# Graph attention on one core: the additive layers as straight code, with the layer norm written per node tile by ScalarE

## The reference

```python
def _L0_gnn_ref(h, W, a, adj):              # layer 2 is the same
    Wh = jnp.einsum('bni,io->bno', h, W)
    s1, s2 = Wh @ a[:Fout, 0], Wh @ a[Fout:, 0]
    e = leaky_relu(s1[:, :, None] + s2[:, None, :], negative_slope=0.2)
    attention = softmax(e + mask(adj)[None, :, :], axis=2)
    return elu(jnp.einsum('bnm,bmo->bno', attention, Wh))

x = _layernorm(x + _L0_gnn_ref(x, L0_gnn_W, L0_gnn_a, adj), axis=-1)
```

## Time and profile before

| | |
|---|---|
| median of 3 runs | 2508.43 us (2503.49 to 2509.16) |
| profiled execution, its time | 2503.22 us |
| profiled execution, its span | 2501.5 us |
| mean granted TensorE clock | 0.913 of full |
| busy: PE, DVE, ACT, POOL | 2154.4, 1853.4, 1133.6, 871.6 us |

### The profile page before, as it was taken

One profiled execution on the slowest core, in us unless ns is written; L12 is line 12 of the kernel. 1 busy time (PEld: TensorE's weight loads), 2 busy tenths in 40 slices (PEclk: granted clock), 3 DMA queues, 4 the chain that ended last, 5 costly groups with the idle time before them and its releaser, 6 DMA issues.

```text
span 2501.5 us, 56118 instructions
## 1 busy us (share of the span) xinstructions
PE 2154.4 (86%) x22776; PEld 1436.9 (57%) x22776; DVE 1853.4 (74%) x2222; ACT 1133.6 (45%) x1992; POOL 871.6 (35%) x631
## 2 busy tenths in 40 slices
PE   6777756788677774999999999999999999999993
PEld 5666646777466663445545555555555555655552
DVE  5888857988588885767786787786776776788773
ACT  3223224443232231655554555564564565556552
POOL 1655644665466553001221222122122122122124
PEclk8888878989788886999998999999998999999997
DMA  5000000000000000000000000000000000000000
GB/s 136 1 0 0 0 1 1 0 0 1 2 1 0 0 0 4 1 9 2 14 14 2 14 14 2 14 13 4 12 13 6 10 13 6 10 14 10 5 14 18
DMA packets 30720, 23.82 MB, mean 10 GB/s; under 512 B 21776, under 2 KB 25424, under 8 KB 30544
## 3 DMA queue, kind: packets, MB, share of 16 engines
q1 hardware_dynamic: 30544, 21.31, 3.5%
HBM read 8.72 MB, written 4.19 MB: 5 GB/s over the span
## 4 chain that ended last, share of the span: by engine, by line
PE 53%; DVE 4%; issue 2%; POOL 1%; ACT 1%; SPq 0%; DMA 0%; DVEq 0%; ACTq 0%; POOLq 0%
PE fourth_ps_out L1331 18%; PE fourth_ps_scores L1283 6%; PE fourth_ps_out L1345 5%; PE fourth_ps_scores L1286 4%; PE fourth_ps_scores L1289 4%; PE fourth_ps_prep L1244 3%; PE fourth_ps_prep L1259 3%; DVE fourth_weights L983 2%; PE fourth_ps_prep L1251 2%; PE fourth_ps_scores L1307 2%; PE fourth_ps_scores L1313 1%; PE fourth_ps_scores L1310 1%; PE fourth_ps_scores L1316 1%; PE fourth_ps_prep L1234 1%; PE fourth_ps_prep L1212 1%
## 5 line engine op out<-in xcount | busy, mean ns | idle before, releaser
L983 DVE TENSOR_TENSOR fourth_weights<-fourth_weights,keep_mask 128x1024 f32<-128x1024 f32 x512 | 681.7, 1371 | 244.4 <-ACT fourth_weights L1131 243.3
L1131 ACT ACTIVATE fourth_weights<-fourth_ps_scores 128x512 f32<-128x512 f32 x1024 | 529.8, 605 | 467.1 <-PE fourth_ps_scores L1289 466.5
L1331 PE MATMUL fourth_ps_out<-fourth_weights,fourth_x_stage 128*64 128x512 f32 x2048 | 498.3, 606 | 1.1 <-DVE fourth_weights L983 1.1
L1331 PEld LDWEIGHTS fourth_ps_out<-fourth_weights,fourth_x_stage 128*64 128x64 f32 x2048 | 123.0, 136 | 235.4 <-issue 186.9
L1283 PE MATMUL fourth_ps_scores<-fourth_g_high,fourth_x_high 64*128 64x512 f32 x1024 | 234.1, 453 | 22.7 <-issue 20.3
L1283 PEld LDWEIGHTS fourth_ps_scores<-fourth_g_high,fourth_x_high 64*128 64x128 f32 x1024 | 98.4, 188 | 221.4 <-issue 121.6
L1289 PE MATMUL fourth_ps_scores<-fourth_g_low,fourth_x_high 64*128 64x512 f32 x1024 | 206.3, 398 | 0.0
L1286 PE MATMUL fourth_ps_scores<-fourth_g_high,fourth_x_low 64*128 64x512 f32 x1024 | 206.2, 397 | 0.0
L990 DVE TENSOR_TENSOR fourth_weights<-fourth_weights,keep_mask 128x1024 f32<-128x1024 f32 x128 | 153.5, 1237 | 66.7 <-ACT fourth_weights L1138 66.7
L404 DVE SCALAR_TENSOR_TENSOR third_weights<-third_row,third_gain,keep_mask 128x1024 f32<-128x1024 f32 x128 | 185.4, 1461 | 12.7 <-ACT third_row L497 10.8
L404 DVE SCALAR_TENSOR_TENSOR first_weights<-first_row,first_gain,keep_mask 128x1024 f32<-128x1024 f32 x128 | 185.0, 1458 | 12.7 <-ACT first_row L497 11.4
(11 more groups left out here) (267 smaller groups left out, 3532.9 us busy)
## 6 DMA issues: line engine op xcount, KB each, us to landing
setup_adj<-in_adj SPq DMA_DIRECT2D x8, 512.0 KB, 7.5
fourth_h_high<-fourth_h_high SPq DMA_DIRECT2D x32, 128.0 KB, 2.3
fourth_h_low<-fourth_h_low SPq DMA_DIRECT2D x32, 128.0 KB, 2.3
out<-keep_x SPq DMA_DIRECT2D x16, 256.0 KB, 2.6
keep_x<-in_x SPq DMA_DIRECT2D x1, 512.0 KB, 11.4
fourth_bias_rows<-in_L_gnn_bh SPq DMA_DIRECT2D x8, 0.2 KB
fourth_wh_in<-in_L_gnn_Wh SPq DMA_DIRECT2D x2, 32.0 KB
fourth_wo_in<-in_L_gnn_Wo SPq DMA_DIRECT2D x1, 64.0 KB
```

Of the source, the lines that this page charges most:

```text
L983: dve.tensor_tensor(buf[:, :], buf[:, :], keep.mask[:, st.t, :].bitcast(F32), ALU.mult)\
L1131: act.activation(weights[st.slot + g][:, cols(half)], ps_scores[g][:, cols(half)], ACT.Exp)\
L1331: last = pe.matmul(ps_out[rows(half), cols(g)], x_stage[st.s][:, st.t, half, :], weights[st.slot + g][:, cols(half)], start=(st.t == 0), s ...
```

## The change

Only `additive_layer` changes, and the norm that it uses. x is turned where it lies, two tiles at a time (4 transposes for 8), so that even tiles come out in the upper and odd tiles in the lower 64 rows; `x_turned` is half as long, and `stage_x` is gone. The new class `NodeNorm` stands for `LayerNorm` in these two layers: ACT squares and sums each tile in one instruction (`accum_out`) with minus the mean as its bias, and writes the normalised x with eight instructions, with rstd as scale and an offset as bias. DVE's reduce over the squares, POOL's `centre` and POOL's write go. y has two buffers. The loop is written out as 16 steps, and no element 16 is prepared. The order on DVE, ACT and POOL changes. `fill_plain` was on POOL and stays there.

```diff
+    def sum_up_squares(self, act, n):
+        act.wait_ge(self.mean_ready, n)
+        for t in range(TILES):
+            act.activation(self.squares[:, t, :], self.y[n % 2][:, t, :], ACT.Square, bias=self.minus_mean[:, t:t + 1],
+                           accum_out=self.sum_squares[:, t:t + 1]).then_inc(self.sum_squares_ready, 1)
+
+    def variance(self, dve, n):
+        dve.wait_ge(self.sum_squares_ready, TILES * n)
+        dve.tensor_scalar(self.variances[:, :], self.sum_squares[:, :], 1.0 / DIM, EPS, ALU.mult, ALU.add)\
+           .then_inc(self.variance_ready, 1)
+
+    def inverse_deviation(self, pool, n):
+
+        pool.wait_ge(self.variance_ready, n)
+        pool.tensor_tensor(self.rstd[:, :], self.variances[:, :], self.exponent[:, :], ALU.pow)\
+            .then_inc(self.rstd_ready, 1)
+        pool.wait_ge(self.rstd_ready, n)
+        pool.tensor_tensor(self.offset[:, :], self.minus_mean[:, :], self.rstd[:, :], ALU.mult)\
+            .then_inc(self.offset_ready, 1)
+
+    def write(self, act, n, x, x_written):
+        act.wait_ge(self.offset_ready, n)
+        for t in range(TILES):
+            act.activation(x[:, t, :], self.y[n % 2][:, t, :], ACT.Identity, bias=self.offset[:, t:t + 1],
+                           scale=self.rstd[:, t:t + 1]).then_inc(x_written, 1)
```

POOL's program:

```diff
+                scale_values(0, 0)
+                for b in range(BATCH):
+                    if b > 1:
+                        norm.inverse_deviation(pool, b - 1)
+                    if b:
                         residual(b - 1)
                     fill_plain(b)
...
+                    if b + 1 < BATCH:
+                        scale_values(b + 1, (b + 1) % 2)
```

DVE's step:

```diff
+                def step(b, s):
                     weigh(b, s, 0)
...
+                    if b > 1:
+                        norm.variance(dve, b - 1)
+                    add_totals(b)
+                    if b:
                         divide(b - 1)
                     weigh(b, s, 1)
...
+                    weigh(b, s, 2)
+                    if b:
                         apply_elu(b - 1)
...
+                    weigh(b, s, 3)
+                    if b + 1 < BATCH:
+                        find_tile_top(b + 1)
+                    weigh(b, s, 4)
+                    if b:
                         norm.mean(dve, b)
...
+                    if b + 1 < BATCH:
+                        find_top(b + 1)
                     weigh(b, s, 5)
...
+                    if b + 1 < BATCH:
+                        copy_tops(b + 1)
                     weigh(b, s, 6)
...
                     weigh(b, s, 7)
```

PE's transposes and its loop:

```diff
+                    for k in range(PAIRS):
+
+                        last = pe.transpose(ps_x[:, k * P:(k + 1) * P],
+                                            keep.x[:, b, 2 * k:2 * k + 2, :].rearrange("p t c -> p (t c)"),
+                                            keep.ident[:, :])
...
+                for b in range(BATCH):
+                    step(b, b % 2)
```

More of the change, by code:

```diff
@@ L255, in additive_layer @@
         elu = sb("elu", [P, TILES, DIM])
-        norm = LayerNorm(mem, "norm", keep.minus_half)
+        norm = NodeNorm(mem, "norm", keep.minus_half)
         ps_x = mem.psum("ps_x")
@@ L460, in _ @@
                 copy_tops(0)
-                step(0, 0, first=True)
-                with dve.Fori(0, (BATCH - 2) // 2) as i:
-                    step(2 * i + 1, 1)
-                    step(2 * i + 2, 0)
-                step(BATCH - 1, 1)
+                for b in range(BATCH):
+                    step(b, b % 2)
+                norm.variance(dve, BATCH - 1)
                 divide(BATCH - 1)
@@ L490, in factors @@
                     act.wait_ge(s1_full, b + 1)
-                    act.activation(above[:, :], ps_s1[:, :], ACT.Relu, bias=tops[:, 1:2]).then_inc(above_ready, 1)
+                    act.activation(above[:, :].rearrange("p (k h q) -> p h k q", h=HALVES, q=P),
+                                   ps_s1[:, :].rearrange("p (h k q) -> p h k q", h=HALVES, q=P), ACT.Relu,
+                                   bias=tops[:, 1:2]).then_inc(above_ready, 1)
                     act.wait_ge(below_ready, b + 1)
@@ L518, in _ @@
                 factors(0, 0)
-                step(0, 0, first=True)
-                with act.Fori(0, (BATCH - 2) // 2) as i:
-                    step(2 * i + 1, 1)
-                    step(2 * i + 2, 0)
-                step(BATCH - 1, 1)
+                for b in range(BATCH):
+                    step(b, b % 2)
+                norm.write(act, BATCH - 1, keep.x[:, BATCH - 2, :, :], x_written)
                 exp_of_negative(BATCH - 1)
-                norm.square(act, BATCH)
+                norm.sum_up_squares(act, BATCH)
+                norm.write(act, BATCH, keep.x[:, BATCH - 1, :, :], x_written)
+                act.wait_ge(x_written, TILES * BATCH)
             @block.tensor
@@ L547, in project @@
                     pe.wait_ge(x_ready, b + 1)
-                    for t in range(PER_BANK):
+                    for k in range(PAIRS):
                         for h in range(HALVES):
-                            last = pe.matmul(ps_x[:, tile_cols(t + h * PER_BANK)], x_turned[rows(h), turned_at(h, t, 1)],
+                            last = pe.matmul(ps_x[:, slot_cols(k, h)], x_turned[rows(h), k * P:(k + 1) * P],
                                              w_aug[rows(h), :], start=True, stop=True)
@@ L610, in _ @@
                 sum_up(0)
-                step(0, 0)
-                with pe.Fori(0, (BATCH - 2) // 2) as i:
-                    step(2 * i + 1, 1)
-                    step(2 * i + 2, 0)
-                step(BATCH - 1, 1)
+                for b in range(BATCH):
+                    step(b, b % 2)
 def dot_layer(nc, stage, keep, ins, out):
```

139 lines of the change are left out of this document (65 added, 74 removed).

## The result

The changed kernel takes 2465.07 us, the median of 4 runs (2458.84 to 2467.13), beside 2506.55 us for the kernel before on the same chip (2503.49 to 2509.16): a ratio of 0.9831 [0.9808, 0.9853]. It is faster by 41 us, 1.7%, where 102 us were forecast, and 2465 lies above the range of 2378 to 2455. The profiled execution spans 2464.3 us, 37.2 less than before.

What follows compares the result with a forecast made beforehand. A step, 19.5 us, was taken as DVE's work plus its waits. Terms 0.65 + 0.8 + 0.7 + 0.3 + 0.1 + 0.9 = 3.45 us off gave 16.1 us; 102 us less, 2406 us, range 2378 to 2455.

Steps and rivals of the forecast that it cites:

- the 4 of the ends: Longer tails of the two layers: +3 us a layer, 6 for both, of which 4 us were kept.
- Point 6: DVE's wait on PE's last multiply, 1.14 us a step, goes if PE's clock is full; net 0.9 us a step.
- the timetable: One step laid out from `copy_tops` at 0 to 16.1 us; PE's longest waits 1.4 us ahead of `multiply` 0, 0.9 for weigh 1.
- The rival's mechanism: PE's clock falls all the same: 2484 us, or 2445 with a fall every second step; chance 0.20.
- point 5: DVE's wait for ACT's row falls from 0.76 to 0.1 to 0.3 us; `values` holds weigh 0 by 0.6; net 0.1 a step.
- Points 1 to 4: DVE gains per step: reduce gone 0.65 us, hold by `centre` 0.8, hold by `plain` 0.7, wait on y less new hold 0.3.
- Point 3: `plain` on POOL now falls beside the reduce of y, not a weigh; hold of 0.7 us a step taken as gone.
- a sign of a wrong forecast: Listed check on DVE: the forecast is wrong if the weighs remain at 1.46 us.
- Point 6's wait on the totals: `add_totals` ahead of the division makes DVE wait for PE, priced at 0.2 us a step.
- 0.81 in the rival: ACT becomes the path: short activations cost 0.81 us each, +1.8 us a step, 2460 us; chance 0.06.
- The written-out loop, "hardly shows": Writing out the additive layers' loop removes register work that hardly shows; no gain was priced for it.
- the rival "code is late": Nothing gained: PE stands 3.8 us a step for late code in the written-out loop, 107 us, 2510; chance 0.04.

Runs made afterwards that it cites:

- pe_fill: The changed kernel with 14 transposes of constants into unused PSUM columns on PE, per element from the third on: 2438.28 us, 0.9725 of the kernel before.
- var_late: The changed kernel with the variance on DVE moved behind the division, no longer ahead of the total: 2436.74 us, 0.9727 of the kernel before.
- div_first: The changed kernel with the division straight behind weigh 0, the variance behind it and the total behind weigh 1: 2406.41 us, 0.9598 of the kernel before.
- norm_old: `div_first` with the old `LayerNorm` (centre and write on POOL, one square on ACT, reduce on DVE): 2463.02 us, 0.9831 of the kernel before.
- straight_only: The kernel before with its loops of steps 1 to 14 in the additive layers written out, nothing else: 2483.21 us, 0.9903 of the kernel before.

## Why the prediction was wrong

The span fell by 37.2 us, where 102.4 (106.4 less the 4 of the ends) were worked out. The 65 us between are 51.0 in the 30 intervals, 4.5 at the ends of the two layers, and 9.7 in other stages that I had at nothing.

**Point 6, "I take the clock as full": the step that failed.** It is the largest part. The pause ahead of multiply 0 was forecast at 1.4 us, is 1.9, and the clock falls behind it in most steps. Intervals with the clock down take 530.4 us, with it up 496.5 (`pe_fill`): 33.9 of the 51.0 us. The rows before could not show that 1.4 us is safe, and I said so, but gave the fall a chance of 0.20. It isn't safe either, with the second pause of the timetable close behind it: at 1.43 and 0.85 us in `var_late` the clock still falls in every second step. "Shorter ones go by at full clock" had too little under it. The earlier trace rows shows no such wait, and the longest that the kernel before has away from the tops is this one, which stands alone and went by at full clock:

```profile
PE first_ps_out L586 <- POOL first_values L321: 4.1, 6, 1.3
```

The rival's mechanism was right, and its two prices, 2484 and 2445, stand on both sides of 2465. In the 28 full intervals of the changed kernel those with the clock down for 6.8 us or more take 17.9 to 19.3 us, and those with it down for 3.4 us or not at all 16.7 to 17.6. The Trainium skill (TensorE: Matmul & The Clock Gate, A second HAM failure mode: psum-queue depth-cycling) speaks of short idles between groups of matmuls that make the clock swing. This trace agrees: 1.90 and 0.78 us of pause, then 0.5 granted. I had weighed that rule as a rival and should have given it more.

**What point 5 and the timetable left out: the squares.** The timetable has no line for the variance's wait. ACT forms them behind the row, from 232.25 to 235.0, 0.33 us from one to the next, and the variance sits in the next step, behind weigh 0. It waits 13.9 us in 15 times; 2.8 of them lie behind the last step, which leaves 0.79 us a step. It also lengthens PE's pause, so it feeds the first error. "The squares lie behind row, 7 us ahead of the time when PE needs the copy behind them" looked at the wrong reader: the one that mattered was DVE, which is through with weigh 0 at 234.24, 1.9 us behind the row's end, while the squares take 2.75. The timetable's own figures had it: row at 2.8, eight squares of 0.3 until 5.2, weigh 0 until 4.7. With the clock up the intervals are 17.1 us over the forecast (496.5 - 479.4); this wait alone costs 22.2 us in the two layers (11.1 in each), and what came out better than priced gives some back. `div_first`, which takes the squares and the total off the chain, goes 4.4 us below the forecast's intervals, 475.0 for 479.4.

**Points 1 to 4.** The reduce and `centre` are gone; `norm_old` measures the reduce at 0.68 us and the hold by `centre` at 0.58 to 0.65 for 0.8. The wait on y went. Point 3 left open whether a reduce is held by `plain`. It isn't, or hardly, as `pe_fill` shows, with weigh 4 held by y (2.20 us for 1.26; I had priced 0.85):

```profile
213.42 2.20 DVE L438 SCALAR_TENSOR_TENSOR first_weights<-first_row,first_gain,keep_mask 128x1024 f32<-128x1024 f32 x1
...
214.50 2.02 POOL L379 TENSOR_TENSOR first_plain<-first_total,keep_no_neighbour 128x512 f32<-128x512 f32 x1
...
215.54 0.67 DVE L160 TENSOR_REDUCE first_norm_sums<-first_norm_y 128x8 f32<-128x512 f32 x1
```

In a step of the changed kernel at half clock weigh 4 starts late and takes 1.57 us, so that part of the hold passes into DVE's wait. That is why the weigh's mean is 1389 ns there; it is 1461 in `pe_fill` (44 to 300 us), for a forecast of 1450. That a weigh would still be at 1.46 us I had called a sign of a wrong forecast. It was not, and could not be one, 10 ns from the forecast: with the clock up it is what the holds by y and `values` come to.

**Point 5, the row**, was better than priced: DVE does not wait for it. **Point 6's wait on the totals**, 0.2 us a step, is 0.3 in all.

**ACT and the ends.** Squares follow each other in 0.33 us and eight writes take 2.76, 0.34 each, for 0.3 forecast and 0.81 in the rival, which fell. The Trainium skill (ScalarE: Activation LUTs, Rules for kernel authors) budgets 0.3 us plus 0.83 ns an element, an estimate of 0.35 us here. The trace agrees for the distance between two starts; a single one lasts 334 ns as a square and 428 as a write. The read-out of 188 ns lies under the next square. The ends of the layers cost 8.5 us: 5.3 inside the stages (55.4 less in the intervals, 50.1 in the layers) and 3.2 in the gaps, where the longer write lies. I had worked out 6 and kept 4; with the old norm, in `norm_old`, the two gaps are at 2.3 and 2.2 us again, from 3.9 and 4.0.

**The written-out loop, "hardly shows".** No fetch gap came into the layers: the rival "code is late" fell there. What I did not see is that the same change moves PE's code in the fourth layer, and that this costs 9.4 us here and gave 13.0 in `straight_only`. With 1.4 us in the second layer and 1.1 back in setup that is 9.7 us.

## What to carry to other kernels

When a change ends one long wait of PE, list every pause that is left and what stands ahead of the instruction that ends it; a pause of 1.4 to 1.9 us with one of 0.8 us close behind it brought the clock down here as the long one did, and the way out was to order the releasing engine's work so that PE's next group comes first. Every step moved to another engine needs its own line in the timetable with its nearest reader, not only with the reader that comes to mind. When a stage that nobody edited changes its time, try a pad of PE instructions ahead of it before crediting or blaming the edit.

## What the runs showed of the hardware

- A short activation with an accumulated output is two instructions: 334 ns and a read-out of 188 ns, overlapped so that 0.33 us lie between starts.
- PE doing 14 transposes more per step made the kernel 27 us faster, with the granted clock at 0.99 for 0.84 over 56 to 300 us.
- Pauses of PE of 1.43 and 0.85 us, with 1.15 us of work between them, brought the clock to 0.5 in every second step (`var_late`); a pause of 1.52 us that stood alone left it up in 24 of 30 intervals (`div_first`).
- DVE's elu took 1.53 us beside a 128x512 operation of POOL and 0.69 alone; DVE's reduce took 0.67 beside one.
- The fourth layer, unchanged, took 1510.8 to 1541.0 us depending on where PE's code lies, and came back to the same time at shifts of 256, 512 and 768 instructions. The Trainium skill (Runtime: NRT & Kernel Launch, Instruction fetch mechanics) says that code is fetched in blocks of 256 instructions, that a jump outside the window held stalls, and that crossing a block is mostly hidden; the runs agree with the block, as far as the shifts go that were run, and with the stall (3.45 and 4.24 us in the rows shown). That the gap of 0.66 us is the crossing of a block is not shown.
- A matmul of one column in fp32 at the start of the second layer cost 0.43 us (the layer took 310.5 us with 128 and 338.0 with 192 of them).
